# A selective-scan layer with a routed feed-forward: row statistics made by ACT instead of VectorE, SiLUs one step sooner, moments and normalizing reordered, one product B x moved from POOL to VectorE

## The reference, cut to what matters

```python
h = (x - mu) / jnp.sqrt(var + 1e-05) * norm_w + norm_b      # x is itself layer-normed before
h = h @ in_proj_w.T
h_conv = sum((hp[:, k:k + L, :] * conv_w[:, k] for k in range(D_CONV)))
h = jax.nn.silu(h_conv)
proj = h @ x_proj_w.T                                       # dt_in, B, C
dt = jax.nn.softplus(dt_in @ dt_proj_w.T + dt_proj_b)
state = jnp.exp(A[None] * dt_t[:, :, None]) * state + B_t[:, None, :] * x_t[:, :, None]
y = jnp.einsum('bnd,bd->bn', state, C_t) + D * x_t
out = jax.nn.silu(y) @ out_proj_w.T + shortcut
x = x + _layernorm(_L0_attn_ref(_layernorm(x, axis=-1), ...), axis=-1)
```

## Time and profile before

| | |
|---|---|
| median of 3 runs | 1411.33 us (1410.96 to 1411.51) |
| profiled execution, own time | 1411.09 us |
| its span | 1409.3 us |
| DVE busy | 1089.8 us |
| POOL busy | 1088.4 us |
| ACT busy | 770.9 us |
| PE busy | 1175.4 us |

### The profile page before, as it was taken

The page is one execution under the profiler, slowest core; times in us unless marked ns, Lnnn a source line. Parts: engine busy times, 40 slices in busy tenths (PEclk is TensorE's granted clock), DMA queues, the critical chain, the costliest instruction groups (busy, mean ns, idle before and its releaser), DMA issues.

```text
span 1409.3 us, 15754 instructions
## 1 busy us (share of the span) xinstructions
PE 1175.4 (83%) x4782; PEld 518.5 (37%) x4783; DVE 1089.8 (77%) x1449; ACT 770.9 (55%) x1275; POOL 1088.4 (77%) x565
## 2 busy tenths in 40 slices
PE   5667678787886987888789688788999999999996
PEld 2222223222321422322233142233556655566653
DVE  3599999999999999999999989799241115776675
ACT  5757468676876866867686686556431111111111
POOL 0489999999999999999999999999122814444553
PEclk9898899999899999989998999999999999999998
DMA  3921211240150122014015012300269522222220
GB/s 108 274 68 62 90 60 32 75 150 0 65 192 1 62 91 106 32 75 149 1 66 175 1 62 90 134 0 31 90 238 324 162 71 82 81 81 79 83 67 15
DMA packets 72075, 127.71 MB, mean 91 GB/s; under 512 B 8759, under 2 KB 48448, under 8 KB 67904
## 3 DMA queue, kind: packets, MB, share of 16 engines
q1 hardware_dynamic: 60432, 103.72, 22.2%
q0 software_dynamic: 7152, 16.81, 3.7%
q10 hardware_dynamic: 4416, 6.29, 1.3%
HBM read 97.79 MB, written 31.76 MB: 92 GB/s over the span
## 4 chain that ended last, share of the span: by engine, by line
PE 36%; POOL 29%; issue 15%; DVE 12%; ACT 8%; DMA 0%; POOLq 0%; ACTq 0%; SPq 0%; DVEq 0%
POOL state L511 18%; PE psX L1647 10%; POOL bx L500 9%; DVE state L1090 6%; PE psX L1582 5%; PE psY L1595 3%; PE psY L1664 2%; PE bank L1664 2%; PE psY L1529 2%; PE bank L1451 2%; POOL lt L516 2%; ACT psX L763 2%; PE bank L1486 1%; DVE bx L1078 1%; DVE acc L1025 1%
## 5 line engine op out<-in xcount | busy, mean ns | idle before, releaser
L511 POOL TENSOR_TENSOR state<-state,cbc 128x1024 f32<-128x1024 f32 x256 | 606.6, 2398 | 14.9 <-DVE state L1090 14.8
L1090 DVE TENSOR_TENSOR_SCAN state<-psX,bx 128x1024 f32<-128x1024 f32 x256 | 578.5, 2279 | 38.5 <-ACT psX L763 23.1
L763 ACT ACTIVATE psX<-dt,aneg 128x511 f32<-128x511 f32 x512 | 330.7, 679 | 199.0 <-DVE state L1090 197.6
L500 POOL TENSOR_TENSOR bx<-xh,bbc 128x1024 f32<-128x1024 f32 x120 | 291.1, 2426 | 59.5 <-DMA bbc<-bc_rows 43.1
L1529 PE MATMUL psY<-state,ident 64*64 64x512 f32 x2048 | 287.5, 654 | 20.3 <-POOL state L511 20.0
L1486 PE MATMUL bank<-prow,ident 128*128 128x512 f32 x272 | 169.9, 710 | 113.3 <-DVE bx L1078 113.3
L1078 DVE TENSOR_TENSOR bx<-xh,bank 128x1024 f32<-128x1024 f32 x136 | 162.7, 1196 | 7.7 <-PE bank L1486 7.6
L1529 PEld LDWEIGHTS psY<-state,ident 64*64 64x64 f32 x2048 | 63.9, 140 | 206.8 <-issue 126.2
L961 ACT ACTIVATE sg<-psX 128x512 f32<-128x512 f32 x39 | 23.3, 597 | 196.5 <-PE psX L1647 196.5
L1486 PEld LDWEIGHTS bank<-prow,ident 128*128 128x128 f32 x272 | 48.0, 209 | 206.9 <-DVE bx L1078 166.9
L581 POOL DMA_INDIRECT ysl<-shared_rows,idx x39 | 40.3, 1033 | 80.6 <-DVE idx L1258 75.9
(11 more groups left out here) (200 smaller groups left out, 1718.8 us busy)
## 6 DMA issues: line engine op xcount, KB each, us to landing
cbc<-bc_rows SPq DMA_DIRECT2D x32, 1024.0 KB, 5.0
bbc<-bc_rows SPq DMA_DIRECT2D x16, 1024.0 KB, 6.2
slot_in<-ao SPq DMA_DIRECT2D x1, 5011.5 KB, 35.1
xsl<-slot_in SPq DMA_DIRECT2D x39, 128.5 KB, 2.0
xin<-in_x SPq DMA_DIRECT2D x8, 512.0 KB, 4.5
xr<-in_x SPq DMA_DIRECT2D x8, 512.0 KB, 5.5
x_rows<-ao SPq DMA_DIRECT2D x8, 512.0 KB, 2.9
xn_rows<-xr SPq DMA_DIRECT2D x8, 512.0 KB, 3.2
```

Of the source, the lines that this page charges most:

```text
L500: nc.gpsimd.tensor_tensor(bx[q % RB][:], xh[par][:, h * CH:(h + 1) * CH], bbc[:, n // 2].unsqueeze(1).broadcast_to([P, CH, L]), ALU.mult). ...
L511: nc.gpsimd.tensor_tensor(w[:], w[:], cbc[:, n].unsqueeze(1).broadcast_to([P, CH, L]), ALU.mult).then_inc(weighted, 1)
L763: e = nc.scalar.activation(decay[q % RD][:, c, 1:L], dt[par][:, h * CH + c, 1:L], ACT.Exp, scale=aneg[:, h * CH + c, n:n + 1])
L1090: nc.vector.tensor_tensor_scan(st[q % RS][:].rearrange("p c t -> p (c t)"), decay[q % RD].rearrange("p c t -> p (c t)"), bx[q % RB][:].rea ...
```

## The change

- `BY_POOL` loses step 12: POOL makes 14 products in a pass, DVE 18.
- The row statistics of x for batches 2 to 7 leave DVE. ACT makes them with eight passes over 256 elements that sum into an accumulator output: four sums at steps 3 to 6, the mean and the first sum of squares about it at step 7, the other three at step 10. Each pass waits for the one ahead. ACT first waits for the load of x at step 3 (DVE waited for it at step 10). The mean then carries the other sign and the variance is left times 256, which `moments` undoes with its scale. The first two batches keep their statistics on DVE.
- `moments(3)` goes from step 29 to 24. In `back`, steps 26 and 27 (moments and norm of the residual) are issued ahead of `front`'s at the same steps (keeping dt).
- The SiLUs and the two table loads go from step 10 to 9. The copy of x's moments goes from step 8 to 6.

```diff
-    BY_POOL = [q % 2 == 0 and q not in (22,) for q in range(Q)]
+    BY_POOL = [q % 2 == 0 and q not in (12, 22) for q in range(Q)]
...
             def lead(f, par, q):
-                if q == 29:
+                def row_pass(k, func, bias, dst):
+                    if k == 0:
+                        act.wait_ge(mv0_ready, f)
+                    else:
+                        act.wait_ge(row_passes, (2 * J - 1) * (f - 2) + k)
+                    nc.scalar.activation(unused[:], xin[:, k % J, :], func, bias=bias,
+                                         accum_out=dst).then_inc(mv0_ready if k == 2 * J - 1 else row_passes, 1)
+
+                if q in (3, 4, 5, 6):
+                    j = q - 3
+                    if j == 0:
+                        act.wait_ge(x_loaded, 16 * (f + 1))
+                    row_pass(j, ACT.Identity, 0.0, xsum[:, j:j + 1])
+                if q == 7:
+                    act.wait_ge(row_passes, (2 * J - 1) * (f - 2) + J)
+                    nc.scalar.activation(mv0[par][:, :, 0], xsum[:], ACT.Identity,
+                                         scale=-1.0 / DIM).then_inc(mean_ready, 1)
+                    act.wait_ge(mean_ready, f - 1)
+                    row_pass(J, ACT.Square, mv0[par][:, 0, 0:1], mv0[par][:, 0, 1:2])
+                if q == 10:
+                    for j in range(1, J):
+                        row_pass(J + j, ACT.Square, mv0[par][:, j, 0:1], mv0[par][:, j, 1:2])
+                if q == 24:
                     act.wait_ge(mv0_ready, f + 1)
-                    moments(3, f, mv0[par], 1.0 + EPS, eps2c)
+                    moments(3, f, mv0[par], (1.0 + EPS) / DIM, eps2c, 1.0)
...
-                if q == 10:
+                if q == 9:
                     act.wait_ge(conv_done, C * (f + 1))
...
+                    if do_back and q in (26, 27):
+                        back(i - 1, q)
                     if do_front:
                         front(i + 1, 1 - par, q)
-                    if do_back:
+                    if do_back and q not in (26, 27):
                         back(i - 1, q)
...
@@ -1106,8 +1139,6 @@
                     if do_front:
                         front(i + 1, 1 - par, q)
-                    if do_lead:
-                        lead(i + 2, par, q)
```

More of the change, by code:

```diff
@@ L123, in build @@
         mv0 = [sb(f"mv0_{i}", [P, J, 2], where=A) for i in range(2)]
+        xsum = sb("xsum", [P, J], where=A)
+        unused = sb("unused", [P, DIM], BF16, where=A)
         mv = [sb(f"mv{i}", [P, J, 2], where=A) for i in range(3)]
@@ L240, in build @@
         mv0_ready = sem("mv0_ready")
+        row_passes = sem("row_passes")
+        mean_ready = sem("mean_ready")
         mv_ready = [sem(f"mv_ready{i}") for i in range(3)]
@@ L612, in _, with moments @@
             ln_exp_tables()
-            def moments(i, b, mvt, scale=1.0, eps=epsc):
+            def moments(i, b, mvt, scale=1.0, eps=epsc, sign=-1.0):
                 nc.scalar.activation(lnv[i][:], mvt[:, :, 1], ACT.Ln, bias=eps[:], scale=scale)
-                nc.scalar.activation(nmr[i][:], mvt[:, :, 0], ACT.Identity, scale=-1.0).then_inc(rs_ready[i], 1)
+                nc.scalar.activation(nmr[i][:], mvt[:, :, 0], ACT.Identity, scale=sign).then_inc(rs_ready[i], 1)
                 act.wait_ge(rs_ready[i], 3 * b + 1)
@@ L698, in back @@
                     act.wait_ge(mv_ready[0], b + 1)
-                    moments(0, b, mv[0])
+                    moments(0, b, mv[0], 1.0 / DIM, epsc, 1.0)
                 if q == 7:
@@ L783, in iteration @@
                         early(q)
[L784 removed]
+                    if q == 9 and (do_front or do_back):
                         ln_exp_tables()
[L786 removed]
+                    if do_scan and q == 6:
                         act.wait_ge(mv0_ready, i + 1)
[L788 to L790 removed]
+                        if isinstance(i, int) and i < 2:
+                            nc.scalar.activation(mv[0][:, :, 0], mv0[par][:, :, 0], ACT.Identity, scale=-1.0)
+                            nc.scalar.activation(mv[0][:, :, 1], mv0[par][:, :, 1], ACT.Identity,
+                                                 scale=float(DIM)).then_inc(mv_ready[0], 1)
+                        else:
+                            nc.scalar.activation(mv[0][:].rearrange("p j a -> p (j a)"),
+                                                 mv0[par][:].rearrange("p j a -> p (j a)"),
+                                                 ACT.Identity).then_inc(mv_ready[0], 1)
                     if do_lead:
@@ L927, in load_group @@
                               xnT_d[LATE_FROM + g]).then_inc(xg_loaded[g % 2], 16)
-            for q in range(10):
+            for q in range(9):
                 back(NB - 1, q)
             keep_y(NB - 1, 1)
-            back(NB - 1, 10)
+            back(NB - 1, 9)
             for c in range(FC):
```

4 lines of the change are left out of this document (2 added, 2 removed).

## The result

The changed kernel takes **1414.87 us** (median of 10 runs, 1412.43 to 1416.03) against 1411.53 for the kernel before, run beside it (10 runs, 1410.3 to 1414.35): 1.0021 times the time, 95% interval 1.0013 to 1.0028. The profiled execution took 1414.73 us with a span of 1412.9; against 1411.09 and 1409.3 that is 3.6 us more, and the traces are compared with each other.

The account below looks back on a forecast made before the run. DVE's work plus its waits for ACT and PE was taken to set the pass. Pass terms +3.1, -1.2, +1.7, -0.3, +0.6, +1.6 gave +5.5, less DVE work +5.3: 1411.1 + 5.3 = 1416.4 us, range 1406.7 to 1422.0.

Parts of the forecast that it names:

- the idle time ahead of the taps in pass 0: Sign of being right: DVE idle for about 3 us ahead of the taps of step 5 in pass 0.
- the wait at scan 0: Sign of being right: DVE's wait at scan 0 falls under 0.5 us.
- the wait ahead of the add to ao: Sign on DVE in the body passes: its wait for PE's out-projection grows from 2.02 to 3.5 to 4 us.
- DVE's own work: Product 12 added, statistics removed: net -0.1 to -0.2 in passes 0 to 5, taken off the sum as 0.2.
- The load of x: Pass 0: ACT stands at step 3 for the load of x, so DVE's taps start later, +3.3 us once.
- dt_in later on PE: PE's dt_in waits behind spread 13, held by product 12: +1.9 in passes 2 to 5, +0.3 to +0.6 in 0, 1, 6.
- rival 1: PE at full rate sooner, dt_in ends near 344.8: +1.9 becomes +0.6 four times, 1411.2; chance 0.12 alone.
- Rival 3: dt_in not held by product 12, so z and out-projection move up: -1.3 in six passes, 1400.1; chance 0.08.
- Products and statistics counted at nothing: DVE loses 1.73 us of statistics, gains 1.5 to 1.6 for product 12: counted 0; POOL's lost 2.43 worth 0.
- Moments: Waits around scan 0 shrink: -0.5 pass 0, -1.5 pass 1, -1.05 passes 2 and 4, -2.05 passes 3 and 5.
- Pass 7 and what follows: No taps at step 9 in pass 7; scan 13 moves from 926.57 to 928.2: +1.6; afterwards 0.
- The port: Rival 2: DVE's 8.26 us minimum in pass 0, cost 4.5: undone 1411.9 (0.10), or in a further pass 1420.9 (0.08).

Follow-up runs that it names:

- run 2: Changed kernel with pass 0's row passes moved to steps 20 to 25 and its moments to step 26: 1411.41 us, 0.9998 to the kernel before.
- Run 9: Changed kernel with POOL waiting at step 22 for DVE's first minimum, and PE's dt_in put ahead of the spread of step 13: 1424.61 us.
- Run 8: Kernel before with the SiLUs at step 9 and POOL waiting at step 22 for DVE's first minimum: 1405.73 us.
- run 11: Changed kernel with step 12 back on POOL, pass 0's row passes at steps 20 to 25, and POOL waiting for DVE's first minimum: 1404.41 us.
- run 3: Kernel before with only moments(3) at step 24 and back ahead of front at steps 26 and 27: 1406.26 us.
- run 10: Kernel before with the SiLUs at step 9, both moves of moments and norm, and POOL waiting for DVE's first minimum: 1402.23 us.
- run 5: Kernel before with POOL's product at step 22 waiting for DVE's first minimum in each pass with a front: 1405.9 us.
- the wait on POOL: Edit holding POOL's step 22 product until DVE's first minimum is done: kernel before 1405.9 us with it, changed kernel 1418.87.
- run 1: Changed kernel with step 12 back on POOL, all else as it is: 1416.2 us, 1.0031 to the kernel before.
- run 4: Kernel before with only the SiLUs and table loads at step 9 in place of 10: 1416.93 us, 1.0027.
- run 12: Same as run 10, but with the SiLUs of pass 7 at step 10: 1405.46 us, in two groups.

## Why the prediction was right, and where its steps were not

The result, 1414.9, is within the range and near the 1416.4; slower by over 0.2% was the likeliest of the three, and it was by a hair. Its steps fared unevenly, and that the sum came so near is in part luck, as the last of them shows. Of the signs that it named, the idle time ahead of the taps in pass 0 came (3.88 us), and the wait at scan 0 went behind passes 2, 4 and 5, with 0.97 left behind pass 3; the wait ahead of the add to ao (3.5 to 4 forecast, 2.36 to 2.46 measured) and POOL's waits (5 to 7 forecast, 4.5 measured) fell short. The sum also took DVE's own work off once, as 0.2, where the 0.1 to 0.2 stood for each of six passes; with 0.6 to 1.2 it comes to 1415.4 to 1416.0.

**The load of x: right.** +3.3 forecast, 3.2 in the trace, 3.5 by run 2.

**dt_in later on PE: the place right, the reason half right, the size right in half of the passes.** Against the taps of step 9 dt_in started 1.9 us later in pass 2 and 3.0 in pass 3. What put it there was PE's own work on one more spread, and not a wait for product 12, which was done before PE came to need it. In passes 3 and 5 the stretch grew by 1.75, close to the 1.9: the spread of step 13 was slow as forecast, and dt_in came 12.6 us after the taps, as forecast (342.2 less 329.55). In passes 2 and 4 it grew by 0.5 to 0.6, because PE was back at the higher level one instruction sooner; that is rival 1, to which I gave 0.12, with the +0.6 worked out for it. The forecast had read the moment of the rise, about 341, off the 4.71 of the earlier trace rows, though the new order put one more spread ahead, and PE so rose by 338.75. I also had the whole price at the add to ao, where in passes 3 and 5 part of it lies at products 15 and 17, whose spreads stand in PE's queue behind dt_in and the rows of B and C. Run 9 shows that this turn of PE's order is no way out.

**Rival 3 falls.** It said that with dt_in free of product 12 the SiLUs a step sooner would gain 1.3 a pass. Run 8 is that case, and it gains nothing: 1405.73 against 1405.9. dt_in is then free of product 12 but still stands behind product 11, and starts at the same time after the taps as before.

**Products and statistics counted at nothing: right as DVE's work, not shown as time.** I set 1.5 to 1.6 for product 12 against 1.73 for the statistics, and DVE's busy time between 320 and 800 us is indeed 448.2 us for 448.8. Product 12 costs 10.5 over eight passes, 1.3 in each, with what it does to dt_in included. But the statistics give nothing back as long as step 12 is on POOL (run 11: +2.2), where POOL is nearly full. Whether they give back their 1.73 when it is on DVE was not run.

**Moments: the mechanism right, 40% too large.** 7.7 forecast for passes 1 to 5, 5.5 measured; run 3 alone gives 5.4, and with the SiLUs and the wait in place (run 10 against run 8) they give 3.5. I had not seen that product 31 would wait 0.49 for its spread and the taps of step 3 some 0.4 for ACT.

**Pass 7 and what follows: +1.6 forecast, +2.8 measured.** The wait of 1.73 behind the SiLUs became one of 2.33 a step earlier, and 0.7 us came behind the last scan, where I had looked at nothing.

**The port: the step that failed.** The forecast left the 8.26 us of the earlier trace rows as it was and gave "undone" 0.17 in all. It was undone, and that is most of the -5.0 in the table. My rival made it hang on the shift of pass 0 by 3.5 us; run 2, where pass 0 lies 3.3 us sooner and the minimum still takes 1.35, speaks against that. What did undo it stays open. The six profiles without the wait on POOL fall one way: the four with step 12 on POOL (the kernel before, runs 1, 3 and 4) have the long minimum in pass 0, the two with it on DVE (the changed kernel, run 2) don't. That is one execution of each, and nothing shows how step 12 would reach the minimum of step 23. My 4.5 for it was too low for pass 0: 5.7 by run 5. The Trainium skill, "SBUF — State Buffer", section "Who interferes with whom", has a DVE instruction with two SBUF inputs contend with a POOL instruction that reads SBUF; the trace agrees, with 1.35 us or 8.25 us for the same instruction. The section also says "Issue order, not op shape, decides who blocks", and the rows here don't bear that out for these two: in each of the long cases the minimum starts about 0.2 us ahead of POOL's product and still is passed by three POOL instructions, and in the short cases of the same kernels it starts the same 0.2 us ahead and goes first.

Had the stall of pass 0 stayed, the changed kernel would have lain at 1419 to 1420 (1414.9 and the 4.5 to 5.0 that the stretch gained), 3 to 4 above the forecast: the side of zero was right, and the sum came out near, by luck, because the missing term and the 2.7 too much in passes 2 and 4 set off what was forecast too low: 2.2 at the moments, 1.2 from pass 7 on, 1.1 in pass 1. With the wait in both, the change costs far more than the result shows, 1418.87 against 1405.9; the 4.0 that the wait itself adds to the changed kernel, which no run explains, is part of that.

## What to carry to other kernels

Two engines that race for one port can hide 5 to 11 us of difference between kernels: look at the longest of a group, not its mean, and try the kernels with a wait that settles the race before anything else is compared. When work is moved to relieve an engine, ask which engine is next to full: here DVE's 1.5 us a pass bought nothing while POOL was busy for 114.3 of 116. And an input that comes sooner is of no use while something else holds the instruction's place in its engine's order: moving the SiLUs ahead couldn't bring dt_in forward while the spread ahead of it waited for product 11. The best kernel found keeps two edits of the change (SiLUs, moments), adds the wait, and leaves products and statistics where they were: 1402.2 us, 0.65% under the kernel before.

## What the hardware showed that I had not expected

- An ACTIVATE over 256 elements that sums into its accumulator shows in the trace as two instructions: 0.41 (Identity) or 0.51 us (Square), then ACTIVATION_READ_ACCUMULATOR, 0.19. From one to the next it is 0.63 us.
- PE's level at the same place differs between executions and between kernels with the same code ahead of it: the first in-projection of pass 0 took 1.98 us in eleven of the fourteen profiles and 3.66 to 3.77 in three, and in the profile of run 12 two such in-projections made up the 4.5 us by which it lay behind run 10.
- A wait that POOL hardly feels (1.16 to 1.25 us in place of a product that was 1.0 longer) was worth 5.6 us to one kernel and cost another 4.0.
